# Attention weights turned by VectorE in squares of 32 and exchanged through DRAM, sums three pairs later

## The reference

```python
xn = layernorm(x, g_in)
q = (xn @ Wq).reshape(b, n, H, DH).transpose(0, 2, 1, 3) * scale   # b=8, n=256, H=16, DH=64
kv = xn @ Wkv
k, v = (kv[..., :DH], kv[..., DH:])          # one key and value head for all 16
k = jnp.concatenate([nk, k], axis=1)          # a fixed key and value in front
v = jnp.concatenate([nv, v], axis=1)
sim = jnp.einsum('bhid,bjd->bhij', q, k) + bias
sim = jnp.where(causal_mask, neg, sim)
sim = jnp.where(mask_p[:, None, None, :], sim, neg)
attn = jax.nn.softmax(sim, axis=-1)
out = jnp.einsum('bhij,bjd->bhid', attn, v)
out = out.transpose(0, 2, 1, 3).reshape(b, n, INNER) @ Wo
return layernorm(out, g_out)
```

## Time and profile before

| | us |
|---|---|
| median of the runs | 797.87 |
| span of the profiled execution | 793.7 |
| attention loop, first to last turning of weights | about 345 to 652 |
| TensorE busy, whole span | 748.7 |
| VectorE busy, whole span | 453.7 |
| ScalarE busy, whole span | 381.9 |
| GpSimd busy, whole span | 422.4 |

### The profile page before, as it was taken

How to read it: one execution, slowest core, us unless ns; L and a number is a source line. 1 busy time by engine, 2 the same in 40 slices (tenths; PEclk the granted TensorE clock), 3 DMA queues, 4 the chain that set the end, 5 groups by cost and what they waited for, 6 DMA issues and landing times. The chain is left out here.

```text
span 793.7 us, 16690 instructions
## 1 busy us (share of the span) xinstructions
PE 748.7 (94%) x4993; PEld 595.9 (75%) x4994; DVE 453.7 (57%) x1647; ACT 381.9 (48%) x1094; POOL 422.4 (53%) x506
## 2 busy tenths in 40 slices
PE   8889999769999999989999999999999988899998
PEld 4479966549999999867777777777777754699965
DVE  0824475672232323356666787778878787256557
ACT  3556612242222222166666565656666651777611
POOL 1077327525554852274656668686868356056640
PEclk9999999759999999999999999999999999999999
DMA  9636635429897773395000000000000001356547
GB/s 323 279 108 191 137 118 160 126 81 342 309 329 273 223 231 121 107 401 174 28 1 28 2 28 29 28 29 28 29 1 29 1 29 63 102 160 177 153 149 236
DMA packets 57022, 106.36 MB, mean 134 GB/s; under 512 B 8816, under 2 KB 42864, under 8 KB 55792
## 3 DMA queue, kind: packets, MB, share of 16 engines
q1 hardware_dynamic: 40368, 55.96, 20.9%
q0 software_dynamic: 10944, 30.03, 12.5%
q10 hardware_dynamic: 5632, 19.41, 7.2%
HBM read 78.31 MB, written 27.07 MB: 133 GB/s over the span
## 5 line engine op out<-in xcount | busy, mean ns | idle before, releaser
L2135 POOL TENSOR_TENSOR work<-work,region_ac 128x386 f32<-128x386 f32 x128 | 120.3, 945 | 67.2 <-DVE work L1797 32.7
L1683 ACT ACTIVATE work<-work 128x129 f32<-128x129 f32 (+1 forms) x256 | 114.0, 449 | 5.8 <-DVE work L1797 5.8
L1797 DVE CUSTOM_DVE_ANT_0 work<-psH,work 128x129 f32<-128x129 f32 (+1 forms) x256 | 78.8, 345 | 2.6 <-PE psH L1482 2.6
L1690 ACT COPY work<-psHT 128x384 f32<-128x384 f32 x64 | 30.6, 479 | 86.4 <-PE psHT L1492 86.4
L1355 POOL DMA_INDIRECT d_pairs<-work,home x47 | 46.1, 981 | 42.8 <-DVE home_f L1107 27.4
L1463 PE MATMUL psY<-work,region_ac 128*128 128x256 f32 x256 | 66.9, 384 | 0.5 <-ACT work L1677 0.5
L1516 PE MATMUL psM<-region_ac,work 128*128 128x256 f32 x256 | 66.0, 380 | 0.0
L1025 ACT ACTIVATE work<-work 128x512 f32<-128x512 f32 x39 | 24.6, 630 | 86.0 <-DVE work L1044 86.0
L1344 POOL DMA_INDIRECT b_pairs<-work,home x39 | 38.0, 975 | 49.8 <-DVE work L1051 46.8
L1336 POOL DMA_INDIRECT work<-in_x,inv x39 | 37.0, 949 | 47.0 <-DVE inv L1264 35.5
L848 PE MATMUL psH<-work,region_bd 128*128 128x128 f32 x472 | 59.2, 280 | 2.0 <-ACT region_bd L747 1.1
(11 more groups left out here) (368 smaller groups left out, 1694.6 us busy)
## 6 DMA issues: line engine op xcount, KB each, us to landing
region_bd<-in_b_w ACTq DMA_DIRECT2D x37, 512.0 KB, 5.4
work<-d_rows SPq DMA_DIRECT2D x47, 132.0 KB, 2.2
a_slots<-work SPq DMA_DIRECT2D x19, 256.0 KB, 2.9
region_bd<-in_b_w SPq DMA_DIRECT2D x1, 4096.0 KB, 15.3
work<-b_pairs SPq DMA_DIRECT2D x16, 256.0 KB, 3.1
region_bd<-in_d_w SPq DMA_DIRECT2D x1, 4096.0 KB, 13.2
work<-d_pairs SPq DMA_DIRECT2D x16, 256.0 KB, 4.3
d_rows<-region_bd SPq DMA_DIRECT2D x1, 2112.0 KB, 28.5
```

The costliest lines, as they stand in the source:

```text
L1683: nc.scalar.activation(c_p[:, o, a:z], c_sc[:, o, a:z], ACT.Exp, scale=-1.0, bias=c_min[:, o, i:i + 1], accum_out=c_sum[:, j % 2, o, i:i + ...
L1797: last = nc.vector.tensor_tensor_reduce(c_sc[:, o, a:z], psH[:, o, a:z], c_bm[:, 2 * (j % 2) + o, a:z], 1.0, -LOWEST, ALU.add, ALU.min, c_ ...
L2135: pool.tensor_tensor(c_bm[:, 2 * (j % 2) + o, :], c_mp, c_bias[:, 2 * j + o, :], ALU.subtract).then_inc(C.bm_ready, 1)
```

## The change

All weights are turned by VectorE: `dve_blocks` transposes them in squares of 32 x 32, one instruction per head with 384 elements per partition, into `c_x1`. A square transposed in place is not a transposed matrix: the squares must still change partitions. SP stores `c_x1` to DRAM (128 rows of 768 floats, `sp_store_blocks`) and loads it again in another order (`sp_load_blocks`, runs of 192 floats) into `c_x2`, from which `pe_sum` reads with a rearranged pattern. The keys are permuted to fit (bias, mask and `c_kT`), and the second fixed key moves to the end. `pe_turn`, `act_pT` and `dve_pT` are gone. Sums, `dve_o` and `pe_out` of a pair come `LAG = 3` pairs later. The reciprocals are taken of the widened sums in one instruction (256 elements), with three buffers, and are still turned by TensorE. Scores alternate between `psH` and `psHT`. `c_x1`, `c_x2`, `c_over` and `c_v` lie where `d_b2` will be, so `d_b2` is loaded after the attention; D's other weights and the pair rows are issued from ScalarE's queue, `d_w2` in eight pieces. The heads of a pair are taken in the order 1, 0, and the steps of the norms move to other pairs.

```diff
         def pe_queries(pe, k, j, odd, b):
-            if live(k, -2, 1 << 30):
-                wait(pe, C.rec_ready, k - 1)
+            if k >= LAG + 1:
+                pe.wait_ge(C.rec_ready, k - LAG)
...
-        def pe_turn(pe, p):
-
-            for o in range(2):
-                pe.wait_ge(C.p_ready, 4 * p + 2 * o + 2)
-                wait(pe, C.pT_ready[o], p)
-                for n, at in enumerate((1, KEYS0 + 1, KEYS0 + 1 + P)):
-                    last = pe.transpose(psHT[:, o, n * P:(n + 1) * P], c_p[:, o, at:at + P], ident[:, :])
-                last.then_inc(C.p_turned, 1)
...
+            wait_dma(pe, C.blocks_loaded, 0, p)
+            weights = c_x2[:, p % 2, :, :, :, :].rearrange("p a o i q -> p o i a q")
+            for n, queries, blocks in ((0, slice(0, SEQ), slice(0, QT)), (1, slice(P, SEQ), slice(QT, QT + 1))):
                 for o in range(2):
+                    last = pe.matmul(psL[DH * o:DH * o + DH, queries].rearrange("p (i a q) -> p i a q", a=4, q=32),
+                                     c_v[:, b % 2, n, :], weights[:, o, blocks, :, :], start=(n == 0), stop=(n == 1))
...
         def dve_sums(dve, p, j):
             dve.wait_ge(C.p_ready, 4 * p + 4)
-            nc.vector.reciprocal(c_rec, c_sum[:, j % 2, :, :]).then_inc(C.rec_done, 1)
+            wait(dve, C.qr_mm, p + LAG - 1 if p >= 3 else 0)
+            nc.vector.reciprocal(c_over[:, p % 3, :, :, :], c_sum[:, j % 2, :, :].rearrange("p o i -> p i o").unsqueeze(3).to_broadcast([P, QT, 2, DH])
+                                 ).then_inc(C.rec_ready, 1)
...
+        def dve_blocks(dve, p, j, o):
+            n = ORDER.index(o)
+            dve.wait_ge(C.p_ready, 4 * p + 2 * n + 2)
+            if p >= 2 and n == 0:
+                wait_dma(dve, C.blocks_stored, 0, p - 2)
+            nc.vector.transpose(out=c_x1[:, p % 2, :, o, :, :].rearrange("p b i q -> p i b q"),
+                                in_=c_p[:, j % 2, o, 1:1 + BLOCK].rearrange("p (i b q) -> p i b q", b=4, q=32)).then_inc(C.blocks_turned, 1)
...
         def dve_batch(dve, b, odd, first, last):
             for j in range(NPAIR):
                 p = 8 * b + j
+                s = p - LAG
+                dve_blocks(dve, p, j, ORDER[0])
                 dve_dispatch_start(dve, b, j, last)
                 if more:
                     dve_scores_wait(dve, p + 1)
+                    dve_scores(dve, p + 1, j + 1, ORDER[0])
+                dve_blocks(dve, p, j, ORDER[1])
                 dve_sums(dve, p, j)
+                if s >= 0:
+                    dve_o(dve, s, s % NPAIR)
-                dve_over(dve, p)
-                dve_pT(dve, p)
                 if more:
+                    dve_scores(dve, p + 1, j + 1, ORDER[1])
...
+        def sp_store_blocks(sp, p):
+            r = p % 4
+            sp.wait_ge(C.blocks_turned, 2 * p + 2)
+            if p >= 4:
+                wait_dma(sp, C.blocks_loaded, 0, p - 4)
+            sp.dma_start(blocks_dram[r].rearrange("a (k b) m -> (a k) (b m)", b=4), c_x1[:, p % 2, :, :, :, :].rearrange("p b o i q -> p (b o i q)")
+                         ).then_inc(C.blocks_stored.sems[p % 2], 16)
+
+        def sp_load_blocks(sp, p):
+            r = p % 4
+            wait_dma(sp, C.blocks_stored, 0, p)
+            wait(sp, C.pv_mm, p - 1)
+            sp.dma_start(c_x2[:, p % 2, :, :, :, :].rearrange("p a o i q -> p a (o i q)"), blocks_dram[r].rearrange("a s m -> s a m")
+                         ).then_inc(C.blocks_loaded.sems[p % 2], 16)
...
         def sp_attention(sp):
-            sp_load_d(sp)
-            with sp.Fori(2, BATCH) as b:
-                sp_pairs(sp, b)
+            sp.wait_ge(fB.y_out, B.NT)
+            sp_clear_rows(sp)
+            sp.dma_start(d_w13, io["d_w13"]).then_inc(D.weights_loaded, 16)
+            pairs = NPAIR * BATCH
+            for p in range(pairs):
+                sp_store_blocks(sp, p)
+                if p >= 1:
+                    sp_load_blocks(sp, p - 1)
+            sp_load_blocks(sp, pairs - 1)
+            sp.wait_ge(C.o_ready, pairs)
+            sp.wait_ge(D.weights_loaded, D.loads)
+            load_broadcast(sp, d_b2, "d_b2", D.weights_loaded)
```

More of the change, by code:

```diff
@@ L280, in build @@
         d_wr = d_wr.rearrange("p (r n) -> p r n", r=DEEP * PAIR)
+        c_x1, c_x2, c_over, c_v = carve(d_b2, [4 * BLOCK, 4 * BLOCK, 3 * SEQ, 2 * QT * DH])
         d_b2 = d_b2.rearrange("p (e n) -> p e n", e=16)
@@ L1443, in build @@
         first_pair = Use(tokens_stored, 1)
+        C.blocks_stored = Use(RingOf((tokens_stored, 0, 2)), NPAIR * BATCH)
+        C.blocks_loaded = Use(RingOf((tokens_stored, 2, 4)), NPAIR * BATCH)
+        tokens_stored.count = C.blocks_stored.after + C.blocks_loaded.after
         def pe_null(pe):
-            pe.wait_ge(C.kT_fixed, 2)
+            pe.wait_ge(C.kT_fixed, 3)
             for j in range(NPAIR):
@@ L1611, in pe_batch @@
                 p = 8 * b + j
-                before = not (first and j == 0)
-                if before:
-                    pe_sum(pe, p - 1, (j - 1) % NPAIR, b - (j == 0))
+                s = p - LAG
                 if not (last and j == NPAIR - 1):
                     pe_scores(pe, p + 1, (j + 1) % NPAIR, b + (j + 1) // NPAIR)
-                pe_turn(pe, p)
+                if s >= 0:
+                    pe_sum(pe, s, s % NPAIR, s // NPAIR)
                 if j == 1 and b >= 3:
@@ L1719, in act_batch @@
                 if more:
-                    act_exp(act, p + 1, j + 1, 1)
+                    act_exp(act, p + 1, j + 1, ORDER[1])
+                act_load_d(act, p)
+                if j == 4 and b + 2 < BATCH:
+                    act_load_pairs(act, b + 2)
                 if j == 5 and not last:
@@ L2036, in dve_batch @@
                 p = 8 * b + j
+                s = p - LAG
                 more = not (last and j == NPAIR - 1)
-                if not (first and j == 0):
-                    dve_o(dve, p - 1, j + 1)
+                dve_blocks(dve, p, j, ORDER[0])
                 dve_dispatch_start(dve, b, j, last)
@@ L2098, in dve_attention @@
             dve_scores_wait(dve, 0)
-            for o in range(2):
+            for o in ORDER:
                 dve_scores(dve, 0, 0, o)
             batches(dve, dve_batch)
-            dve_o(dve, NPAIR * BATCH - 1, NPAIR - 1)
+            for j in range(NPAIR - LAG, NPAIR):
+                dve_o(dve, NPAIR * (BATCH - 1) + j, j)
             dve_key(dve, BATCH - 2, psX)
@@ L2131, in pool_bm @@
         def pool_bm(pool, b, p, j, o):
-            if j == 0 and o == 0:
+            if j == 0 and o == ORDER[0]:
                 pool.wait_ge(C.mask_ready, 2 * b + 2)
-            wait(pool, C.score_ready, 2 * p + o - 3)
+            wait(pool, C.score_ready, 2 * p + ORDER.index(o) - 3)
             pool.tensor_tensor(c_bm[:, 2 * (j % 2) + o, :], c_mp, c_bias[:, 2 * j + o, :], ALU.subtract).then_inc(C.bm_ready, 1)
@@ L2205, in pool_batch @@
                 over = (j + 2) // NPAIR
-                for o in range(2):
-                    h = 2 * j + o
+                for n, o in enumerate(ORDER):
+                    h = 2 * j + n
                     if h <= 2 * QT and not last:
                         pool_pairs_wait(pool, b + 1, h)
-                    if j == 4 and o == 0:
+                    if j == 4 and n == 0:
                         pool.wait_ge(C.xn_ready, 2 * b + 2)
-                    if j == 6 and o == 1 and not first:
+                    if j == 6 and n == 1 and not first:
                         pool.wait_ge(C.z_step, 2 * b)
@@ L2492, in _ @@
             dve_attention(dve)
+            dve.wait_ge(D.weights_loaded, D.loads + 16)
             dve_ffn_pairs(dve, fD)
```

203 lines of the change are left out of this document (102 added, 101 removed).

## The result

The changed kernel takes 855.21 us (median of 4 runs, 854.9 to 858.48) against 798.28 us for the kernel before on the same chip: 1.0757 times as long, 95% interval 1.0703 to 1.081. The forecast was 843 us, slower, with 815 to 905 as its range. The ratio and its interval are estimated from the fast runs of both kernels, so they are not exactly the quotient of the two medians (1.071); 797.87 us, given above as the time before, is the median of the first three of the same four runs. The profiled execution spans 853.2 us where the one before spanned 793.7: 59.5 us more.

A forecast was written before the change was run, and what follows sets the result against it. TensorE bounds the attention stage before, VectorE after. The stage's +38 us, 2 at the start and 5 at the end make 45 us on 797.9, so 843 us, range 815 to 905.

The forecast's parts named there:

- VectorE, added (a), the reciprocal: In `dve_sums`, one reciprocal over 256 elements per pair: 1.75 us taken, bounds 0.42 and 2.11 us.
- Rival 1: TensorE stays the bound because the wide reciprocal on VectorE costs like a copy; 760 us, chance 0.08.
- VectorE, added (b), the turnings: Two VectorE transposes in squares of 32 per pair, 384 elements each: 0.55 us apiece, bounds 0.35 and 0.945.
- VectorE's busy time: Attention stage: 2.61 us a pair added, 0.95 removed, so VectorE's busy time goes from 228 to 333 us.
- The waits: VectorE's unavoidable idle time in the stage: 6 us for exponentials and 6 us for GpSimd's power.
- the start: VectorE's third pair waits for the first store to DRAM: 1 to 3 us, taken as 2.
- the tail: End of the attention: one store, load, sum, product and output after the last turning, +5 us.
- Exchange: Store and load through DRAM, about 3.5 us per transfer, hidden in the steady state, showing only at the ends.
- 4: Rival: the DRAM exchange binds, deciding at 7 us a transfer; at 9 us the kernel takes 950, chance 0.04.
- 3: Rival: TensorE's granted clock drops; with half of the stage at the low level, 887 us, chance 0.04.
- rival 2: VectorE's two added costs are off, the mechanism holds: 818 to 915 us; chance 0.82 together with the forecast.
- TensorE's relief: Six transposes per pair leave TensorE, 0.71 us a pair, 45 us, lowering its need to about 259 us.

The follow-up runs named there:

- e4: Changed kernel with the product `dve_o` issued on VectorE ahead of the long reciprocal; ratio 1.0507 to the kernel before, 883.4 us against 841.37.
- e1: Changed kernel with the 4-element reciprocal and widening copy back on VectorE, reciprocal ahead of the second half's turning; ratio 1.0116 to the kernel before, 847.52 us against 841.37.
- e2: Kernel before with only the 256-element reciprocal in place of small reciprocal and widening copy; ratio 1.0698 to the kernel before, 897.95 us against 841.37.
- e5: Changed kernel storing and loading only 192 of the 768 floats per partition through DRAM; ratio 1.0709 to the kernel before, 902.75 us against 841.37.
- e3: Changed kernel with a 4-element reciprocal on VectorE and the widening copy on ScalarE; ratio 0.9878 to the kernel before, 0.9895 when repeated on another chip.
- e9: e3 with the variances of the rows moved right behind their moments; ratio 0.9828 to the kernel before, 825.8 us against 843.26.

## Why the prediction was right, point by point

**Which engine.** Right. The change makes VectorE the busiest engine (324 of 361 us), and the loss is VectorE's: some 40 us of it by its own work, as e4 shows, in which it is 97% busy, and some 20 by what it keeps waiting.

**VectorE, added (a), the reciprocal.** The term that carried the forecast: 1.753 us from the slope between 4 and 16 elements, measured 1.710. Three lengths of one instruction (178 ns, 253 ns, 1710 ns) lie on a line of 6.1 to 6.3 ns per element. The upper bound of 2.11 us, and the nearby 2.1 us estimated from the Trainium skill (page "VectorE: DVE Perf Modes", section "Walkthrough: the 8-slice pipeline in each mode"), were both too high; that page's mechanism, a divide that repeats per element, fits the row, its count does not. Rival 1 fell with this number. e1 (319.7 us of attention without it, 375.6 with it, 314.9 before) and e2 (368.0 with it alone) show that this one instruction is nearly the entire loss.

**VectorE, added (b), the turnings.** 0.55 us taken from the copy of as many elements, measured 0.572. The 0.93 us that the prediction scaled from the figure of the Trainium skill, same page, section "The three transpose paths", did not hold here.

**VectorE's busy time.** Forecast 333 us, measured 323.7. The reciprocal and the turnings together are 182.4 us for 64 pairs, 2.8 more than the forecast's 2.85 x 63 = 179.6. The products are 4.5 us less in sum (26.1 us before, 21.6 after): 0.36 us each in the steady state of the kernel after, 0.42 before and in its last three; before, also the 22 that had not waited for the sums took no less than 0.408, and the cause is open. Normalising rows is 5.6 us more (14 x 880 ns, not 488), and other small passes are about as much less. The rest, some 8 us, is left by subtraction; it would be more overlap between instructions that follow each other without a wait, but it was not measured.

**The waits, the step that failed.** Forecast 12 us in which VectorE is idle: 6 for exponentials, 6 for GpSimd. Measured 37.4: GpSimd's 5.8 as forecast, 0.5 for exponentials, the first store's landing 4.9 (2 had been taken, counted as the start), and 24.0 for scores. For these the forecast had nothing, without a reason given: it took the scores as there when VectorE comes to them. The prediction went through VectorE's order instruction by instruction to sum it, and did not ask who waits for what stands behind the long one. That is `dve_o`, and through `pe_out` the next scores. It was findable beforehand: `dve_sums` stands ahead of `dve_o` in the changed `dve_batch`, and its length goes from 0.18 to 1.75 us by the prediction's own figure. e4 shows the loop at about 20 us. e2 shows a relative of it in the other kernel, where TensorE waits for the long instruction's own result.

**Where 45 became 59 in the profiled span.** From the first marks to the last turning the forecast had 38 + 2 = 40 us; the last turning starts 51.1 us later (652.9 to 704.0). Behind it 5 had been forecast, 12.5 - 4.2 = 8.3 came. 51.1 + 8.3 = 59.4 of the 59.5. VectorE's busy time was sized 9 too high, its waits with the start's 2 counted in 23 too low (14 against 37.4), the tail 3 too low. These add to 17, of which 3 go again because the first turning starts 1.5 us earlier and the last marks lie a little differently. So a part of the errors cancelled, and that the forecast came within 14 us is in part luck. The tail was costed as one chain of store, load, sum, product and output; with sums three pairs late there are three such chains. The median rose by 56.9 us, some 3 less than the profiled span.

**Exchange, clock, `d_b2`.** Hidden in the steady state, as e5 shows: a store of 384 KB landed in 2.7 us and a load in 3.7 by the median (the forecast: about 3.5), for the forecast's 11 us of room. The first store took 10.7 us to land, behind `d_w13`, which stays on SP's queue (the text on the change gives all other weights of D to ScalarE's queue, which holds but for this one), and VectorE waited 4.9 us for it. The clock: 0.98 from 400 us on, 0.96 over the stage. Reading the weights in runs of 32 costs TensorE next to nothing: in the steady state the matmuls of the sums take 409 and 275 ns in the mean (256 and 128 columns), before 405 and 273. What the later `d_b2` costs was not tried.

**Rivals.** 1 and 4 are out by the reciprocal's length and by e5. 3 supposed half of the stage at the low level; the clock was 0.96 in the mean, and what is left of this rival are 12 us at the start. What rival 2 called "some wait I did not see, each 0.2 us a pair is 13 us" is what happened: 24 us of waits against 9 less work.

**What TensorE's relief is worth, the second term that was off.** The forecast counted 0.71 us a pair, 45 us in all, off TensorE and left it a need of 4.11 us a pair, 259 us. It was not the bound, so this did not move the forecast, but e1 was expected by it and missed. Over the attention of before, after and e3 (answers to the earlier trace rows):

```profile
342.20:657.10 314.90, 309.97 (x2256) 229.63 (x2256) 232.00 (x1028) 193.76 (x676) 206.28 (x261) 1.00 0.14 50
340.90:716.50 375.60, 293.02 (x1872) 199.31 (x1872) 329.03 (x1028) 174.96 (x614) 208.55 (x262) 0.96 0.55 173
339.00:645.90 306.90, 279.73 (x1872) 196.00 (x1872) 243.08 (x1028) 187.23 (x678) 207.56 (x262) 0.97 0.67 211
```

TensorE's busy time fell by 17 us in the kernel after and by 30 in e3, not by 45. The same matmuls are recorded as longer where TensorE no longer runs without gaps: those of `pe_out` 380 ns in the mean in the stage before, 411 after. How much of that is the gaps, the lower clock of the start, or the way their ends are modelled was not separated. From the fourth batch on e3 takes 37.5 us a batch of 8 pairs (from reciprocal to reciprocal), 4.7 a pair, of which TensorE is busy 4.4, against 39.5 us for the kernel before. So e3's attention is 8 us shorter than before and not 45: 15 of the missing 37 us are work that did not go, and 22 are idle time of TensorE, 27.2 us now where it was 4.9. e9, which also moves the variances, is 16 us shorter.

## What to carry to other kernels

Before two instructions are merged, look for a length of the merged kind at two sizes in the profile: here 178 and 253 ns for 4 and 16 elements told that the reciprocal pays 6 ns an element, so to invert few values and then copy them wide (on the idle engine) is cheap, to invert them wide is not. When an instruction gets longer, costing it as busy time is half the work: go through what is queued behind it on its engine and who waits for that, and if the other engine is near its bound too, put the result that it waits for first. And a bound engine that is relieved need not give back what its blocks measured in the timeline: here 8 to 16 us came of the 45 that were counted, in part because its busy time fell by 30 only, in part because it now waits for its neighbour.

## What was not expected of the hardware

- The two new instructions hardly vary: the turning 564 to 580 ns over 128 times, the reciprocal 1701 to 1711 over 64.
- Normalising rows (128 x 256, VectorE) takes 488 ns in the mean before and 880 after, with no change to it. The widening copy of e1 varies too: 25 of its 64 take over 0.6 us and 5 over 1.0. Each of these 25 runs while GpSimd is in an instruction, mostly its pass over 386 elements (line 2164), and the 12 copies that meet no work of GpSimd take 0.24 to 0.25 us. That points to GpSimd, but about half of the copies that meet its work are not longer, its records are rough, and no run tested it: the cause stays open.
- The kernel before takes 841 and 843 us on two chips, 792 on a third, and took 798 in the first result. The kernel after was profiled on two: spans of 853.2 and 905.6 us, of which the attention differs by 2 us, what lies ahead of it by 31 and what lies behind it by 19.
- TensorE at 79% of a stretch (236.6 of 300 us) kept a granted clock of 0.98; at 46% (5.54 of 12 us) it had 0.77. But e4, busy 86% of the same stretch (258.8 of 300 us), had 0.94, so the busy share of a stretch alone does not tell its clock.
